# Routing lists of a top-2 mixture of experts: one-hot rows that carry the token number, gate weights kept in the token table, output rows sent during attention

## The reference

```python
h = h + _L1_attn_ref(_layernorm(h, axis=-1), Wq, Wk, Wv)
h = h + _L1_ffn_ref(_layernorm(h, axis=-1), Wr, W1, b1, W2, b2)

def _L1_ffn_ref(x, Wr, W1, b1, W2, b2):          # 8 experts, top 2, hidden width 768
    gate_logits = x_flat @ Wr
    topw, topi = jax.lax.top_k(gate_logits, 2)
    topw = jax.nn.softmax(topw, axis=-1)
    combine = combine.at[arange(T)[:, None], topi].add(topw)
    h = relu(einsum('td,edh->eth', x_flat, W1) + b1[:, None, :])
    y = einsum('eth,ehd->etd', h, W2) + b2[:, None, :]
    out = einsum('te,etd->td', combine, y)
```

## Time and profile before

| | us |
|---|---|
| median of three runs (lowest, highest) | 935.53 (931.87, 936.73) |
| the profiled execution | 933.64 |
| its span in the profile | 931.9 |
| TensorE busy, share of the span | 769.3, 83% |
| VectorE | 554.8, 60% |
| ScalarE | 421.8, 45% |
| GpSimd | 362.7, 39% |

### The profile page before, as it was taken

One profiled execution on the slowest core, in us unless ns is written; L12 is line 12 of the kernel. 1 busy time (PEld: TensorE's weight loads), 2 busy tenths in 40 slices (PEclk: granted clock), 3 DMA queues, 4 the chain that ended last, 5 costly groups with the idle time before them and its releaser, 6 DMA issues. The chain is left out here.

```text
span 931.9 us, 23842 instructions
## 1 busy us (share of the span) xinstructions
PE 769.3 (83%) x8368; PEld 649.7 (70%) x8369; DVE 554.8 (60%) x1399; ACT 421.8 (45%) x1068; POOL 362.7 (39%) x392
## 2 busy tenths in 40 slices
PE   3689999999977866555789999915599999999993
PEld 3577888888865544344557778705599999999993
DVE  2698888787752212111667777789466555565562
ACT  4566776676632211111125777544144444444441
POOL 1433443434321000000114788328655555555552
PEclk8799999999966977877769999955699999999997
DMA  9309100000025999999256000063123333333331
GB/s 262 107 25 428 60 2 2 2 2 3 2 87 185 399 423 427 427 425 415 73 218 262 2 1 1 1 161 89 63 45 53 52 50 49 49 50 50 52 50 17
DMA packets 35035, 118.16 MB, mean 127 GB/s; under 512 B 7619, under 2 KB 24421, under 8 KB 30597
## 3 DMA queue, kind: packets, MB, share of 16 engines
q1 hardware_dynamic: 24100, 104.30, 29.5%
q0 software_dynamic: 10848, 12.67, 8.5%
HBM read 105.77 MB, written 11.14 MB: 125 GB/s over the span
## 5 line engine op out<-in xcount | busy, mean ns | idle before, releaser
L1878 POOL DMA_INDIRECT out_h<-x_ys,idx x55 | 87.5, 1591 | 98.1 <-ACT x_ys L1903 86.2
L2002 PE MATMUL psum<-w_pairs,x_h_hi 128*128 x330 | 101.8, 371 | 1.3 <-DVE x_h_lo L1930 1.1
L2004 PE MATMUL psum<-w_pairs,x_h_lo 128*128 x330 | 82.6, 250 | 0.0
L1930 DVE TENSOR_TENSOR x_h_lo<-psum,x_h_hi 128x384 fp32r<-128x384 f32 x110 | 56.3, 553 | 39.2 <-ACT x_h_hi L1899 39.1
L521 POOL TENSOR_SCALAR a_u<-flat,a_mv 96x192 f32<-96x192 f32 x32 | 24.2, 757 | 133.9 <-DVE a_mv L693 133.9
L1903 ACT ACTIVATE x_ys<-x_ys,cw 128x192 f32<-128x192 f32 x55 | 25.1, 456 | 102.3 <-DVE x_ys L1941 102.3
L1899 ACT ACTIVATE x_h_hi<-psum 128x384 fp32r<-128x384 f32 x110 | 48.1, 489 | 37.7 <-PE psum L1991 37.6
L2002 PEld LDWEIGHTS psum<-w_pairs,x_h_hi 128*128 128x128 f32 x330 | 61.9, 188 | 3.6 <-issue 3.6
L2004 PEld LDWEIGHTS psum<-w_pairs,x_h_lo 128*128 128x128 f32 x330 | 63.0, 191 | 0.0
L1865 POOL DMA_INDIRECT x_xg<-xtab,idx x55 | 55.1, 1002 | 16.6 <-issue 16.1
L1166 POOL MEMSET f_hid<- 96x96 f32 x1 | 0.2, 179 | 152.7 <-PE psum L1234 152.7
(11 more groups left out here) (282 smaller groups left out, 2250.4 us busy)
## 6 DMA issues: line engine op xcount, KB each, us to landing
flat<-in_slot_w SPq DMA_DIRECT2D x23, 2304.0 KB, 31.9
ring<-in_slot_w SPq DMA_DIRECT2D x8, 2304.0 KB, 31.0
flat<-in_moe_w SPq DMA_DIRECT2D x1, 10752.0 KB, 29.5
flat<-in_x_patches SPq DMA_DIRECT2D x4, 1536.0 KB, 13.1
flat<-in_slot_w SPq DMA_DIRECT2D x4, 576.0 KB, 32.9
out_h<-flat SPq DMA_DIRECT2D x1, 2304.0 KB, 12.3
xtab<-flat SPq DMA_DIRECT2D x4, 576.0 KB, 4.0
m_y<-in_fc_b SPq DMA_DIRECT2D x4, 384.0 KB, 7.2
```

Source lines behind the costliest of these rows:

```text
L1878: pool.indirect_dma_start(out=A["out"][:, :], out_offset=bass.IndirectOffsetOnAxis(ap=g.idx[:, i:i + 1], axis=0), in_=ys[:, i % 2, :], in_ ...
L1930: v.tensor_tensor(h_lo[:, 3 * n:3 * n + 3, :], b_hT[n], h_hi[:, 3 * n:3 * n + 3, :].bitcast(F32), ALU.subtract).then_inc(s_hl, 1)
L2002: pe.matmul(b_y[u % 2], h_hi[:, k, :], g.w_pairs[:, :, k, bass.ds(e, 1), :].rearrange("p two a d -> p two (a d)"), start=(k == 0), stop=False)
L2004: mm = pe.matmul(b_y[u % 2][:, 1, :], h_lo[:, k, :], g.w_pairs[:, 1, k, bass.ds(e, 1), :].rearrange("p a d -> p (a d)"), start=False, stop ...
```

## The change

Routing lists:

- The token number is now 1 + token, and it goes into the one-hot rows: `tokens` holds, for each of a pass's 8 columns, (iota equals row) times token number, made by one `tensor_scalar` of 96x128 per column with two per-partition scalars, instead of one wide comparison per pass. `info` shrinks to its first plane, `occ`, padded to 56 columns. The planes for token number and both weight halves go, and GpSimd's part in the loop with them. The matmul has 56 columns instead of 220. A sum under 0.5 marks a place without a pair.
- The gate weights are not put into the lists. The table row grows by four floats (`DX` 256 to 260): two numbers that tell the pair's experts (expert − 8) and two weights. Four more transfers of 16 bytes per token write them, issued by SP after the third quarter of rows, behind a wait for the weights. In the tile loop a new step `pick` on VectorE compares the two numbers with the tile's expert (`te_less`), multiplies with the weights and adds the two. The gather waits for `pick` of four tiles before (`s_cw`), where it waited for the turn (`s_xTp`).
- The three operations that finish the weights move behind `place` in VectorE's chain.
- Counts, sums and tile experts are computed on 128 partitions instead of 96.

Output rows:

- SP stores `g.h` into the output in four parts during attention, each behind `keep` of its eight sequences. The bias is loaded ahead of `moe_w`.
- ScalarE normalises a quarter when its part has been stored, written out without a loop; the exponential comes before sequence 16.
- In the tile block GpSimd's first two gathers come ahead of the filling of the constant row, which now fills all 128 partitions, and VectorE waits for it.

```diff
-DX = 4 * 64
+DX = 4 * 64 + 4
@@ attention1, SP
+            sp.dma_start(g.b1s[:, :], A["moe_b1"].rearrange("e (q f) -> (e q) f", f=NE * F // 128)).then_inc(g.s_b1, 16)
             sp.dma_start(g.flat[:, 0:NW], A["moe_w"]).then_inc(g.s_e, 16)
+            rows = A["out"][0:NTOK, :].rearrange("(b t) d -> t b d", t=T)
+            for c in range(B // PART):
+                part = slice(c * PART, (c + 1) * PART)
+                sp.wait_ge(s_keep, (c + 1) * PART)
+                sp.dma_start(rows[:, part, :], g.h[:, part, :]).then_inc(g.s_kept[c], 16)
@@ route, SP
-            sp.dma_start(A["out"][0:NTOK, :].rearrange("(b t) d -> t b d", t=T), g.h[:, :, :]).then_inc(s_h, 16)
-            sp.dma_start(b1s[:, :], A["moe_b1"].rearrange("e (q f) -> (e q) f", f=NE * F // 128)).then_inc(s_b1, 16)
...
                 sp.dma_start(rows[:, part, 0:D], g.h[:, part, :]).then_inc(s_tab, 16)
-                sp.dma_start(rows[:, part, D:DX], g.h[:, part, 2 * 64:D]).then_inc(s_tab, 16)
-            sp.wait_ge(s_tab, 10 * 16)
+                sp.dma_start(rows[:, part, D:DX - 4], g.h[:, part, 2 * 64:D]).then_inc(s_tab, 16)
+                if q == NQ - 2:
+                    sp.wait_ge(s_gates, 2)
+                    for c in range(NQ):
+                        some = slice(c * B // NQ, (c + 1) * B // NQ)
+                        sp.dma_start(rows[:, some, DX - 4:DX], gates[:, some, :]).then_inc(s_tab, 16)
+            sp.wait_ge(s_tab, 14 * 16)
@@ route, GpSimd
-            pool.memset(ones[:, :], 1.0).then_inc(s_ones, 1)
...
-            for q in range(NP):
-                pool.wait_ge(s_occ, q + 1)
...
-                pool.tensor_tensor(info[:, q % 2, :, 1, :], occ, tokid[:, cols].unsqueeze(2).broadcast_to([T, PART, NTILES]),
-                                   ALU.mult).then_inc(s_info, 1)
...
@@ route, ScalarE
-            act.wait_ge(s_h, 16)
-            with act.Fori(0, B // UNROLL) as j:
...
+            for b in range(B):
+                if b % (B // NQ) == 0:
+                    act.wait_ge(g.s_kept[b * NQ // B], 16)
+                if b == B // 2:
+                    act.wait_ge(s_d, 1)
+                    act.activation(ex[:, 0, :], ex[:, 0, :], ACT.Exp).then_inc(s_ex, 1)
+                act.activation(g.h[:, b, :], g.h[:, b, :], ACT.Identity, scale=g.rstd[:, b:b + 1],
+                               bias=g.nmr[:, b:b + 1]).then_inc(s_norm, 1)
@@ route, VectorE
+            v.wait_ge(s_ex, 1)
+            link(v.tensor_scalar(ex[:, 1, :], ex[:, 0, :], 1.0, None, ALU.add))
+            link(v.reciprocal(gates[:, :, 2], ex[:, 1, :]))
+            v.tensor_tensor(gates[:, :, 3], ex[:, 0, :], gates[:, :, 2], ALU.mult).then_inc(s_gates, 2)
...
             for q in range(NP):
                 cols = slice(PART * q, PART * q + PART)
                 if q >= 2:
                     v.wait_ge(s_part, q - 1)
...
+                v.tensor_tensor(occ[:, q % 2, :, :], iota[0:T, 0:NL].unsqueeze(1).broadcast_to([T, PART, NL]),
+                                wide(flat(tile)[:, cols], NL), ALU.is_equal).then_inc(s_tokens, 1)
+                for j in range(PART):
+                    col = PART * q + j
+                    v.tensor_scalar(tokens[:, q % 2, j, :], iota[0:T, :], flat(row)[:, col:col + 1],
+                                    tokid[:, col % B:col % B + 1], ALU.is_equal, ALU.mult).then_inc(s_tokens, 1)
...
+            link(v.tensor_scalar(lst[:, 0, :], b_list, 0.5, None, ALU.is_lt))
+            link(v.scalar_tensor_tensor(lst[:, 1, :], lst[:, 0, :], padrow[:, 0:1], b_list, ALU.mult, ALU.add))
+            link(v.tensor_scalar(g.idx[:, :], lst[:, 1, :], -1.0, None, ALU.add))
@@ route, TensorE
             for q in range(NP):
-                pe.wait_ge(s_ohp, 2 * q + 2)
-                pe.wait_ge(s_info, 2 * q + 2)
+                pe.wait_ge(s_tokens, (1 + PART) * (q + 1))
                 for j in range(PART):
-                    mm = pe.matmul(b_list, ohp[:, q % 2, j, :], info[:, q % 2, j, :, :], start=(q == 0 and j == 0),
+                    mm = pe.matmul(b_sums, tokens[:, q % 2, j, :], occ[:, q % 2, j, :], start=(q == 0 and j == 0),
@@ expert_tiles, GpSimd
-            pool.memset(one[:, :], 1.0).then_inc(s_mem, 1)
-            pool.wait_ge(s_mem, 1)
-            pool.tensor_copy(x_lo[64:128, 1, :], one[64:128, :]).then_inc(s_one, 1)
...
-                        pool.wait_ge(s_xTp, t - NX + 1)
+                        pool.wait_ge(s_cw, t - NX + 1)
...
+                if t == 1:
+                    pool.memset(one[:, :], 1.0).then_inc(s_mem, 1)
+                    pool.wait_ge(s_mem, 1)
+                    pool.tensor_copy(x_lo[:, 1, :], one[:, :]).then_inc(s_one, 1)
+                    pool.wait_ge(s_one, 1)
@@ expert_tiles, VectorE
+            v.wait_ge(s_one, 1)
+            def pick(i, u):
+                item(v, s_xTp, i)
+                numbers, weights = xg[:, u, DX - 4:DX - 2], xg[:, u, DX - 2:DX]
+                v.scalar_tensor_tensor(picked[:, :], numbers, g.te_less[:, bass.ds(i, 1)], weights, ALU.is_equal,
+                                       ALU.mult).then_inc(s_pick, 1)
+                item(v, s_pick, i)
+                v.tensor_reduce(g.cw[:, bass.ds(i, 1)], picked[:, :], AX.X, ALU.add).then_inc(s_cw, 1)
...
-            steps(v, NTILES, [(relu, 1), (x_rest, 0), (turn_rest, 1), (add_bias, 2)])
+            steps(v, NTILES, [(relu, 1), (pick, 0), (x_rest, 0), (turn_rest, 1), (add_bias, 2)])
```

More of the change, by code:

```diff
@@ L178, in build @@
         g.s_add = sem("s_add")
+        g.s_kept, g.s_b1, g.s_rones = [sem(f"s_kept{c}") for c in range(4)], sem("s_b1"), sem("s_rones")
         g.s_ring = [sem(f"s_ring{i}") for i in range(NU)]
@@ L1794, in _ @@
+            v.tensor_scalar(g.te_less[:, :], tef[:, :], float(-NE), None, ALU.add)
             v.wait_ge(s_list, 1)
[L1796 to L1800 removed]
+            link(v.tensor_scalar(lst[:, 0, :], b_list, 0.5, None, ALU.is_lt))
```

132 lines of the change are left out of this document (52 added, 80 removed).

## The result

The changed kernel takes 929.11 us (median; 926.43 to 933.41), the kernel before 934.35 us on the same chips: a ratio of 0.9949, 95% interval 0.9937 to 0.9961. It is faster, by 5.2 us instead of the 12.9 forecast. The forecast of 922.6 us started from 935.53, the median of three runs; with 934.35, that of twenty, it would have been 921.4. The profiled execution took 929.3 us, its span is 927.5 (before 931.9).

What follows compares the result with a forecast made beforehand. VectorE's list loop was taken to bound routing, TensorE the tiles. Terms +0.4 − 0.1 − 11.3 − 1.5 − 0.4 = −12.9 us, from the median 935.53 to 922.6 us; own range 918 to 929, opened to 917 to 932.

Steps and rivals of the forecast that it cites:

- What bounds the kernel: Tile loop bound by TensorE, 40.00 of 40 us busy; routing stage by VectorE, 29.50 of 29.50, its slowest chain paid in full.
- Attention, head, tail: Attention +0.4 us, head of routing −0.1, tail behind the list loop −1.5, TensorE's last pass covering the tile-expert operations.
- The list loop: Routing's eight passes at 2.14 us each, eight `tensor_scalar` at 0.20: 17.1 us instead of 28.43, −11.3 (−13.2 to −6.2).
- Rival D: One-operation rows no cheaper: 0.35 us a column, a pass 3.34, the loop 26.7 us, the kernel 932.2; chance 0.12.
- The tile start: First gather earlier, but GpSimd's weight pieces remain and tile 1's `pick` may meet them: −0.4 us (−1.4 to +1).
- Rival C: Steady tiles: `pick` overruns its 0.80 us gap, held by GpSimd's scatter issue; +0.4 × 55 = +22, so 944.6; chance 0.10.
- Rival B: Gate transfers set the routing stage's end; at 80 ns a piece it is 5.2 us longer, kernel 927.8; chance 0.12.
- the cover: Routing: normalisations start at 607.1 instead of 619.65, so weight splits end near 638.8, 5.5 us under the lists.
- 24 ns a piece: Cost to a DMA engine of each gate-transfer piece, taken from 256-byte pieces; adds 4.6 us in series before the splits.
- The trace disagrees: Against the skill's warning on transfers under 512 B: 256-byte pieces cost 24 ns against 43; no 16-byte store shown.

Runs made afterwards that it cites:

- the series: Changed kernel with extra blocks behind its end: VectorE operations on own data, some beside GpSimd arithmetic, with or without a gather ahead; holds 0.50 to 6.18 us.

## Why the prediction was right or wrong

- **What bounds the kernel**: right. The loop is VectorE's alone, the steady tiles are TensorE's, and what was saved in the loop came through.
- **Attention, head, tail**: right, 0.1 us off or less by the table of stages. The last pass is covered as said.
- **The list loop**: the mechanism is right (GpSimd silent, 0.54 for the occupancy, TensorE's eight at 1.91 against 1.9 said, VectorE setting the pace), the price of one `tensor_scalar` is wrong. This step failed: it was put at 0.20 as "the first slope with a bit over one pointer charge"; the operation has two pointers. The columns and the overlap were right: 0.14 was the end without pointers, and eight such operations take 1.17 us, 0.14 to 0.15 each. Two charges of 0.06 make 0.26. The term is −7.7 instead of −11.3: 3.6 us of the miss. The range (0.14 to 0.28) held the value; the choice inside it was the fault, since both pointers can be read off the diff: its own 50 ns, charged twice, would have given 0.24.
- **Rival D** had the direction: dearer operations, at 0.26 instead of its 0.35, because they do overlap.
- **The tile start**: the other step that failed is "may meet those pieces. −0.4 (−1.4 to +1)". The meeting was seen and left a place in the range, but none in the term. The start became 3.2 us longer, outside that range: the hold went over the end of a piece, `x_rest` of tile 1 and TensorE's first layer stood behind it, and that layer then ran at the lower clock (2.5 and 1.1 us against the kernel without the step). With the step out, or the hold out, the start is 14.0 to 14.4 us, so the −0.4 without the meeting was right (14.67 in one kernel without a hold, where the clock rose later): 3.6 us of the miss.
- **Rival C** named this mechanism, but for the steady tiles. There it does not happen: GpSimd only issues gathers and row adds, `pick` takes 0.21 us beside a 1.59 us issue, and the steady tiles are equal with and without the step. The idle time ahead of `x_rest` is shortened, not gone, as the prediction asked.
- **Rival B**: not so. The splits end 9.0 us under the lists. Without the early store they would have ended 0.4 us over them: the cover was real, and the 24 ns a piece was near (some 20). "The trace disagrees" says too much, though: 24 ns for 256 bytes against 43 for 768 is less a piece, but 0.094 against 0.056 ns a byte, so the rows do show small pieces to be dearer by their bytes.
- **Sum**: −12.9 + 3.6 + 3.6 = −5.7, measured −5.2 by the medians. The traces' −4.4 hold 0.6 from a stage that was not changed, and 0.75 from the long last line of the table, of which no run shows a cause: kernels with the same tile stage (the changed one, the one with wide operations, the one with the store undone) take 243.95 to 245.74 us from the first to the last row add. That the time of 929.1 us lies inside the stated 917 to 932 is owed to the width of the range: the two failed steps add up, and nothing in the sum made good for them.

The Trainium skill, "SBUF — State Buffer", section Who interferes with whom, has the two engines exclude each other "for the whole instruction". Without a gather ahead the series agree: all 17 holds end with the instruction that was met. Behind a gather most do not: 3.26 to 7.45 us over instructions of 1.5 to 1.8 us.

## What to carry to other kernels

Price an operation by its operands as well as its columns, and count every pointer: many narrow operations with pointers can lose to one or two wide ones. A small step that is free in the steady loop can be dear in the prologue: look at what stands beside it there, above all at GpSimd's arithmetic right behind its own gathers, and give that work a wait between its parts or move it. Add to a wait of TensorE what the lower clock costs behind it. A step belongs into a gap of its engine and not into a chain that comes round: the same 0.36 us cost nothing in the one and 0.7 us a tile in the other.

## What the runs showed of the hardware

- A `tensor_scalar` of 96x128 on VectorE takes 0.14 us from start to start without pointers, 0.20 with one and 0.26 with two; 128 more columns add 0.07.
- A two-column operation with one input in SBUF and two pointers is held by GpSimd's arithmetic like one with two inputs (1.07 and 1.06 us); a reduction of two columns is not (0.14).
- GpSimd operations right behind its own gather kept a VectorE operation with two inputs in SBUF out to the end of the fourth and last of them: 3.72, 6.18, 5.79, 3.72 and 5.16 us in the series, 3.26 (three kernels) and 7.45 us in kernels. With waits between them it got in after the one that it met (1.45, 0.91 and 1.73 us), and so it did after a wait for the gather's landing (0.74, one arrival). One case stays open: with the step alone in the kernel before, which also has gathers ahead of its pieces, VectorE was let in at the end of a piece (0.33 us).
- TensorE's granted clock, at 1.00, fell to 0.50 for some 3.4 us after a wait of 2.47 us; matmuls of the first layer then came 0.32 us apart instead of 0.17.
- 3072 stores of 16 bytes in four transfers moved the end of ScalarE's splits by some 3.8 us (an estimate, by two kernels that differ in more) where the splits had no cover; with it the splits ended 9.0 us before they were needed.
